# Splitting the keys of four attention blocks per image, in a three-layer attention kernel on one core

## The chip, the core and the metric

The kernel runs on one core of a Trainium2 chip. Five engines work side by side: TensorE (PE, its weight loads PEld), VectorE (DVE), ScalarE (ACT), GpSimd (POOL) and SyncE (SP), which issues most transfers. They meet only at semaphores. The metric is the device time of one execution in microseconds.

## The reference

The input is two images of 32 by 32 tokens with 128 channels. Three layers follow one another, each with a residual:

```
x = LN(x + gate * proj(neighbourhood attention 7x7, 8 heads))   # per image, zero-centred q, k, v
u = LN(x);  h = tanh(q[i] + k[j] + bh), 32 units wide
t = x + softmax_j(h . Wa) @ u                                    # all 1024 keys j of the image
t = t + FFN of one expert in eight, chosen by argmax of LN(t) @ gate_w, capacity 320 tokens
```

The middle layer is the costly one: for each query and each of 1024 keys of its image a tanh over 32 hidden units, 2 x 1024 x 1024 x 32 values. The first layer needs for a block of 128 tokens (4 image rows) the keys of at most 10 rows. The middle layer needs the first layer's result of all the image's tokens as keys, and of one block as queries.

## The kernel before, in words

Tokens are cut in 16 blocks of 128, eight to an image.

**Rounds.** The first layer runs in rounds rho = 0 to 31, two for a block (even and odd heads). A round is: four score products on TensorE (L601), four biased scores with their minimum on VectorE (`bias_score`, L1125), four exponentials on ScalarE (L986), two or three groups of four transposes (L630 or L639), their copies (L993, L1144, L1152), and value products (L648). After a block's second round the heads are normalized, projected and gated. Rounds 0 to 15 (image 0) run by themselves at the start.

**The passage.** Then the layer norms of rows 4 to 7 run on VectorE in one chain (`row_stats`, `scale_start`, `scale_end`, `normal_rows`, `weigh_rows`), tokens are transposed (`turn_tokens`), and the keys k4 and the queries q4 are projected.

**Units.** The middle layer runs in 128 units, eight to a block. A unit is a tile `ring[t % 3]` of 128 x 4096: four tiles of 1024 keys, each with another query column q4[:, m] added. GpSimd adds to keys in SBUF (`key_query_sums`, L507) and VectorE to a copy of the keys in PSUM (L1323): in image 0 GpSimd writes 2 x 1024 + 2 x 512 columns and VectorE 2 x 512; in image 1 GpSimd 2 x 1024 + 512, VectorE 512 + 1024. ScalarE takes one tanh over all 4096 columns (L1049), and TensorE sums over the hidden units (`energies`, L801) into PSUM banks 0 and 1. Sums for unit t are written while step t - 2 runs, and may not overtake `h_used` of unit t - 3.

**The end of a block.** After its eighth unit VectorE takes the minimum over 1024 energies (`least`, L1330; TensorE waits for it before the next block's first energies), ScalarE the exponential (L1053), TensorE transposes and attends (L813, L822), and VectorE normalizes, routes and numbers the tokens (L1349 to L1393) over the next steps. GpSimd scatters the record (L515).

**The order.** Every engine's program is one loop over steps t. Fixed functions of t say what it does: `begin(rho) = 3 * (rho - 17)` starts rounds 16 to 31 every third step, from -3 to 42, and `values_step`, `project_step` and `query_block` follow from it and from the block's end. Image 1's layer norms of rows 12 to 15 lie at steps 49 to 55 or so, and its keys have to be there at unit 64. After unit 127 the expert layer runs.

## Time and profile before

| | us |
|---|---|
| median of 3 runs | 742.11 |
| lowest, highest | 741.74, 746.65 |
| the profiled execution | 744.08 |
| its span | 741.9 |

The span is that of one profiled execution, from its first to its last instruction; 2.2 us of that execution's time lie outside. Busy shares are PE 77%, ACT 78%, DVE 75%, POOL 63%. The execution has four parts: the first image's rounds and the passage up to the first tanh at 109.8 us; units 0 to 63 with the second image's rounds between them, up to 421.8; units 64 to 127, up to 659.9; and the expert layer.

### The profile page before, as it was taken

To read this page: it belongs to the slowest core of one execution; us is meant where nothing else is said; L and a number is where in the kernel's file an instruction comes from. 1 tells how busy PE (TensorE), PEld (TensorE's weight loads), DVE (VectorE), ACT (ScalarE), POOL (GpSimd) and SP (SyncE) were. 2 spreads that over 40 slices of the span, in tenths; PEclk is the share of its full clock that TensorE was granted. 3 is DMA by queue.
4 is the path that set the end of the run, shared out by engine and by line. 5 is a ranking of instruction groups with operands and counts; after the bars stand their busy time and mean duration, and the time that the engine had idled before them with its cause. 6 is when DMAs were issued, how large, how long until landed. Compare 5 with 4: busy or idle time off the path is not lost.

```text
span 741.9 us, 12240 instructions
## 1 busy us (share of the span) xinstructions
PE 570.2 (77%) x4496; PEld 272.5 (37%) x4496; DVE 555.0 (75%) x1444; ACT 577.5 (78%) x368; POOL 470.6 (63%) x539
## 2 busy tenths in 40 slices
PE   6999858798999868899447666766767668768994
PEld 3666423243434323343113131222222212328783
DVE  3768765768897768878987788798798786853356
ACT  3777539998999767899457899999999999960541
POOL 2000228976888668788835788788888886830464
PEclk9999968999999869999858899999999998986998
DMA  8500000000000000007000000000000000001400
GB/s 322 175 1 2 1 0 2 0 2 4 9 4 10 3 9 5 1 12 285 21 4 8 4 11 2 12 9 4 12 10 4 12 8 5 6 7 25 133 22 28
DMA packets 13819, 22.22 MB, mean 30 GB/s; under 512 B 1264, under 2 KB 11026, under 8 KB 12992
## 3 DMA queue, kind: packets, MB, share of 16 engines
q1 hardware_dynamic: 12352, 18.53, 7.3%
q0 software_dynamic: 1408, 2.91, 1.2%
q8 instruction: 36, 0.59, 0.3%
q14 instruction: 23, 0.19, 0.1%
HBM read 14.70 MB, written 7.37 MB: 30 GB/s over the span
## 4 chain that ended last, share of the span: by engine, by line
PE 36%; DVE 27%; issue 18%; ACT 13%; POOL 4%; DMA 0%; DVEq 0%; POOLq 0%; SPq 0%; ACTq 0%
PE ps L801 12%; ACT front L1049 11%; DVE front L1323 7%; POOL front L507 4%; PE ps L601 3%; PE ps L946 3%; PE ps L936 2%; PE ps L648 2%; PE ps L822 2%; DVE back L1125 2%; PE ps L630 2%; PE ps L639 2%; DVE lnw L134 1%; PE ps L813 1%; DVE rec L1362 1%
## 5 line engine op out<-in xcount | busy, mean ns | idle before, releaser
L507 POOL TENSOR_SCALAR front<-k,q 128x1024 f32<-128x1024 f32 (+1 forms) x448 | 410.9, 936 | 129.0 <-PE ps L801 110.7
L1049 ACT ACTIVATE front<-front 128x4096 f32<-128x4096 f32 x128 | 456.2, 3608 | 41.8 <-DVE front L1323 23.6
L801 PE MATMUL ps<-front,cst 128*32 128x512 f32 x2048 | 277.1, 648 | 74.8 <-ACT front L1049 61.1
L1323 DVE TENSOR_SCALAR front<-ps,q 128x512 f32<-128x512 f32 (+1 forms) x256 | 213.5, 877 | 34.6 <-PE ps L801 27.9
L801 PEld LDWEIGHTS ps<-front,cst 128*32 128x32 f32 x2048 | 53.1, 114 | 173.6 <-issue 85.2
L986 ACT ACTIVATE back<-back,mn 128x320 f32<-128x320 f32 (+1 forms) x128 | 62.5, 537 | 20.2 <-DVE mn L1125 20.2
L1125 DVE CUSTOM_DVE_ANT_0 back<-ps,back 128x320 f32<-128x320 f32 (+1 forms) x128 | 54.0, 468 | 12.8 <-PE ps L601 11.8
L464 POOL TENSOR_SCALAR y_all<-y_all,lny,lnc 128x128 f32<-128x128 f32 x8 | 3.5, 444 | 69.0 <-DVEq L1224 69.0
L1338 DVE COPY ptm<-ps 128x512 f32<-128x512 f32 x32 | 22.1, 689 | 30.1 <-PE ps L813 30.1
L1152 DVE COPY back<-ps 128x512 f32<-128x512 f32 x44 | 30.2, 687 | 16.3 <-PE ps L639 13.9
L639 PEld LDWEIGHTS ps<-cst,back 128*128 128x128 f32 x176 | 20.0, 150 | 44.0 <-issue 31.6
L832 PE MATMUL ps<-cst,rec 128*128 128x128 f32 x16 | 5.9, 371 | 38.0 <-DVE rec L1362 38.0
L822 PEld LDWEIGHTS ps<-x_one,ptm 128*128 128x128 f32 x256 | 31.4, 199 | 10.0 <-issue 8.8
L822 PE MATMUL ps<-x_one,ptm 128*128 128x129 f32 x256 | 34.3, 289 | 0.8 <-DVE ptm L1338 0.8
L515 POOL DMA_INDIRECT xbuf<-rec,slots x16 | 16.3, 1019 | 29.2 <-DVEq L119 25.9
L639 PE MATMUL ps<-cst,back 128*128 128x128 f32 x176 | 31.3, 303 | 2.2 <-DVE back L1152 2.0
L543 POOL DMA_INDIRECT out<-back,dest x20 | 19.9, 993 | 17.6 <-DVE back L1529 13.4
L630 PE MATMUL ps<-cst,back 128*128 128x128 f32 x176 | 27.3, 287 | 1.7 <-ACT back L993 1.7
L601 PE MATMUL ps<-late 32*128 32x320 f32 (+1 forms) x128 | 26.7, 494 | 2.5 <-DVE mn L1125 1.7
L813 PEld LDWEIGHTS ps<-cst,pm 128*128 128x128 f32 x128 | 14.7, 151 | 32.8 <-issue 19.2
L813 PE MATMUL ps<-cst,pm 128*128 128x128 f32 x128 | 22.9, 306 | 4.7 <-ACT pm L1053 2.0
L1072 ACT ACTIVATE front<-ps 128x384 f32<-128x384 f32 (+1 forms) x8 | 3.1, 434 | 29.8 <-PE ps L926 29.8
(140 smaller groups left out, 701.4 us busy)
## 6 DMA issues: line engine op xcount, KB each, us to landing
back<-in_w SPq DMA_DIRECT2D x2, 2048.0 KB, 10.3
xbuf<-rec SPq DMA_DIRECT2D x1, 2720.0 KB, 14.4
front<-xbuf SPq DMA_DIRECT2D x2, 720.0 KB, 7.2
back<-in_inner SPq DMA_DIRECT2D x1, 1280.0 KB, 9.8
back<-in_b SPq DMA_DIRECT2D x1, 1280.0 KB, 14.1
xT<-in_xT SPq DMA_DIRECT2D x4, 256.0 KB, 5.4
back<-in_top SPq DMA_DIRECT2D x1, 1024.0 KB, 6.8
back<-in_bottom SPq DMA_DIRECT2D x1, 1024.0 KB, 14.9
```

The costliest lines, as they stand in the source:

```text
L507: last = nc.gpsimd.tensor_scalar(ring[t % 3][:, c, lo:hi], k4[:, img * L + lo:img * L + hi], q4[:, m:m + 1], 1.0, ALU.add, ALU.mult)
L601: return nc.tensor.matmul(bank(to, 0, n), q_par[img][r][rows, at * P:(at + 1) * P], kT[img][rows, k0:k0 + n], start=True, stop=True)
L630: last = nc.tensor.transpose(bank(turn_bank(rho, c), g * P, (g + 1) * P), prob[r][:, g, c * P:(c + 1) * P], c_("ident"))
L639: last = nc.tensor.transpose(bank(4, g * P, (g + 1) * P), prob[rho % 2][:, g, c * P:(c + 1) * P], c_("ident"))
L801: last = nc.tensor.matmul(bank(half)[c * U:(c + 1) * U, :], c_("wa", U - QPG - QPG * s, 2 * U - QPG - QPG * s), ring[t % 3][:, c, half * 5 ...
L813: last = nc.tensor.transpose(bank(4, k * P, (k + 1) * P), pm[:, (4 * half + k) * P:(4 * half + k + 1) * P], c_("ident"))
L822: last = nc.tensor.matmul(bank(6, 2 * P, 2 * P + C + 1), ptm[:, k, :], x_one[:, p // BPI * BPI + k, :], start=(k == 0), stop=(k == BPI - 1))
L986: nc.scalar.activation(prob[r][:, g, 0:n], nlog[r][:, g, 0:n], ACT.Exp, bias=mn[r][:, g:g + 1], scale=-1.0).then_inc(p_ready, 1)
L1049: nc.scalar.activation(ring[t % 3], ring[t % 3], ACT.Tanh).then_inc(h_ready, 1)
L1125: nc.vector.tensor_tensor_reduce(out=nlog[r][:, g, 0:n], in0=bank(frm, 0, n), in1=btab[kind][:, 2 * g + r, :], scale=-1.0, scalar=3e38, op ...
L1152: nc.vector.tensor_copy(pts[rho % 2][:, c, :], bank(4)).then_inc(turn_copied, 1)
L1323: last = nc.vector.tensor_scalar(ring[t % 3][:, c, lo:hi], ps[:, at + lo:at + hi], q4[:, m:m + 1], None, ALU.add)
```

## The change: what it does

- Only rounds 0 to 11 run by themselves. Rounds 12 to 31 lie in the step loop, which begins at step -6, at steps given by a table: -6, -3, 0, 2, then 7 to 35 every fourth, then 38 to 59 every third.
- The units are cut in groups. In each image blocks 0 to 3 first take the 512 keys of the image's first half (four units a block, eight tiles of 512 keys), then, again four units a block, the other 512; blocks 4 to 7 take all keys as before. So units 0 to 15 need only the tokens of blocks 0 to 3; the second half's keys are made at step 14 and used from unit 16. There are 128 units as before. In image 1 the first half's keys are made at step 61 and the second's at about 75.
- Energies of a half group go to one bank, block by block in turn, and TensorE waits for the minimum of the group before the last rather than of the last. The minimum and the shifted energies of the first half are kept in `pmh` and `nmh`; the exponential is in two instructions then.
- In second halves ScalarE makes the eighth tile itself, from the keys with the query as its bias, so a unit has a tanh of 3584 columns and one of 512, and VectorE has one sum less.
- In half units GpSimd writes six tiles of 512 in image 0 and five in image 1; VectorE two and three, less the one of ScalarE in second halves.
- Layer norms of rows 0 to 3 come earlier among the rounds. Those of rows 4 to 6 and of row 7 are separate chains inside steps 7 to 12, on VectorE, with rows 4 to 6 weighed by GpSimd.
- q, k and v of the first layer have one buffer (`conv`) instead of two, overwritten at steps 4 to 9.

```diff
-PACE = 3
+RS = 12
+BS = RS // 2
...
+BEGIN = dict(zip(range(RS, NR), [-6, -3, 0, 2] + [7 + 4 * k for k in range(8)] + [38 + 3 * k for k in range(8)]))
+ROWS_STEPS = (7, 8, 9)
+ENTRY = 4
+KEYS_1, TOKENS_2, KEYS_2 = 14, 58, 61
...
+        self.block, self.half, self.first, self.units = block, half, first, units
+        self.last = first + units - 1
+
+
+GROUPS = []
+for _img in range(B):
+    for _half in range(2):
+        for _k in range(BPH):
+            GROUPS.append(Group(_img * BPI + _k, _half, len(GROUPS) and GROUPS[-1].last + 1, CH // 2))
+    for _k in range(BPH, BPI):
+        GROUPS.append(Group(_img * BPI + _k, None, GROUPS[-1].last + 1, CH))
+GROUP_AT = [n for n, g in enumerate(GROUPS) for _ in range(g.units)]
+FINAL = {g.block: n for n, g in enumerate(GROUPS) if g.half != 0}
+PEND = [GROUPS[FINAL[p]].last for p in range(NB)]
+
+
+def tiles_of_unit(u):
+
+    g = GROUPS[GROUP_AT[u]]
+    k = u - g.first
+    base = g.block * U
+    if g.half is None:
+        return [(c * L, 0, L, base + c * CH + k, k, c) for c in range(QPG)]
+    return [(n * HL, g.half * HL, HL, base + n % QPG * CH + 2 * k + n // QPG, 2 * k + n // QPG, n % QPG)
+            for n in range(2 * QPG)]
...
+def leasts_before(n):
+
+    return n if GROUPS[n].half is None or (n and GROUPS[n - 1].half is None) else n - 1
...
-        late = sb("late", [P, 3 * L + VB * NH * HP])
-        q_par, kT, vals = [], [], []
-        for t in (front, late):
-            q_par.append([t[:, r * L:(r + 1) * L] for r in range(2)])
-            kT.append(t[:, 2 * L:3 * L])
-            vals.append(t[:, 3 * L:3 * L + VB * NH * HP].rearrange("p (n h d) -> p n h d", n=VB, h=NH))
-        ring = [front[:, i * QPG * L:(i + 1) * QPG * L].rearrange("p (c j) -> p c j", c=QPG) for i in range(3)]
+        conv = sb("conv", [P, 3 * L + VB * NH * HP])
+        q_par = [conv[:, r * L:(r + 1) * L] for r in range(2)]
+        kT = conv[:, 2 * L:3 * L]
+        vals = conv[:, 3 * L:3 * L + VB * NH * HP].rearrange("p (n h d) -> p n h d", n=VB, h=NH)
...
+        NEW_KEYS = [0, 4 * BPH, T // 2, T // 2 + 4 * BPH]
+
+        def pool_part(u, n):
+
+            g = GROUPS[GROUP_AT[u]]
+            if g.half is not None:
+                return (0, HL) if n < (6 if g.block < BPI else 5) else (0, 0)
+            if g.block < BPI:
+                return (0, L) if n < 2 else (0, HL)
+            return (0, L) if n < 2 else (0, HL) if n == 2 else (0, 0)
+
+        def biased(u):
+
+            return GROUPS[GROUP_AT[u]].half == 1
...
+                if u in NEW_KEYS:
+                    pool.wait_ge(k4_ready, 1 + NEW_KEYS.index(u))
+                    pool.wait_ge(q4_ready, 1 + NEW_KEYS.index(u))
+                for n, (at, k0, keys, m, _, _) in enumerate(tiles_of_unit(u)):
+                    lo, hi = pool_part(u, n)
+                    if lo < hi:
+                        last = nc.gpsimd.tensor_scalar(ring[u % 3][:, at + lo:at + hi],
+                                                       k4[:, img * L + k0 + lo:img * L + k0 + hi], q4[:, m:m + 1],
+                                                       1.0, ALU.add, ALU.mult)
                 last.then_inc(pool_sums, 1)
...
+                if t == 8:
+                    scale_rows(2, 4, 7)
+                    weigh_rows("lng", ALU.mult, 4, 7)
+                    weigh_rows("lnb", ALU.add, 4, 7, done=True)
+                if t == 11:
+                    normal_rows(2, 4, 7)
...
+                    if t == g.first and leasts_before(n) > 0:
+                        pe.wait_ge(least_ready, leasts_before(n))
+                tiles = tiles_of_unit(t)
+                for at, _, keys, _, row, c in (tiles if keys_whole(t) else tiles[half * QPG:(half + 1) * QPG]):
+                    to, at = (half, at + half * HL) if keys_whole(t) else (g.block % 2, at)
+                    last = nc.tensor.matmul(bank(to)[c * U:(c + 1) * U, :],
...
+                if t == begin(RS) + 1:
+                    spread(BS - 1)
+                    turn_tokens(0, 0)
+                if t == begin(RS) + 2:
+                    project(BS - 1)
+                    key_half(0, 5)
+                    query_columns(0, 1)
...
+                if t == KEYS_1:
+                    pe.wait_ge(n_ready, NG * (RPI + 2))
+                    turn_tokens(1, 2)
+                    query_columns(1, 3)
+                    pe.wait_ge(dve_sums, NEW_KEYS[1])
+                    key_half(1, 5)
...
+                if biased(t):
+                    at, k0, keys, m, _, _ = tiles_of_unit(t)[-1]
+                    k0 += GROUPS[GROUP_AT[t]].block // BPI * L
+                    if t in NEW_KEYS:
+                        act.wait_ge(k4_ready, 1 + NEW_KEYS.index(t))
+                        act.wait_ge(q4_ready, 1 + NEW_KEYS.index(t))
+                    nc.scalar.activation(ring[t % 3][:, 0:at], ring[t % 3][:, 0:at], ACT.Tanh)
+                    nc.scalar.activation(ring[t % 3][:, at:at + keys], k4[:, k0:k0 + keys], ACT.Tanh,
+                                         bias=q4[:, m:m + 1]).then_inc(h_ready, 1)
+                    return
...
+                    nc.scalar.activation(pm[:, 0:HL], pmh[:, p % BPI, :], ACT.Exp, bias=nmin[:, :], scale=-1.0)
+                nc.scalar.activation(pm[:, lo:L], pm[:, lo:L], ACT.Exp, bias=nmin[:, :], scale=-1.0).then_inc(pm_ready, 1)
...
+                if half is None and img == 0:
+                    base -= HL
+                if half == 1 and img == 0:
+                    base -= HL
+                for n, (at, k0, keys, m, _, _) in enumerate(tiles_of_unit(u)):
+                    lo = pool_part(u, n)[1]
+                    if lo < keys and not (biased(u) and n == 2 * QPG - 1):
+                        last = nc.vector.tensor_scalar(ring[u % 3][:, at + lo:at + keys],
+                                                       ps[:, base + k0 + lo:base + k0 + keys], q4[:, m:m + 1], None, ALU.add)
                 last.then_inc(dve_sums, 1)
...
+                if g.half == 0:
+                    k = p % BPI
+                    if p >= BPI:
+                        dve.wait_ge(pm_ready, k + 1)
+                    nc.vector.tensor_tensor_reduce(out=pmh[:, k, :], in0=bank(p % 2), in1=c_("ba").broadcast_to([P, HL]),
+                                                   scale=-1.0, scalar=3e38, op0=ALU.add, op1=ALU.min,
+                                                   accum_out=nmh[:, k:k + 1]).then_inc(least_ready, 1)
...
+                if g.half == 1:
+                    link(nc.vector.tensor_tensor_reduce(out=pm[:, HL:L], in0=bank(p % 2), in1=c_("ba").broadcast_to([P, HL]),
+                                                        scale=-1.0, scalar=3e38, op0=ALU.add, op1=ALU.min,
+                                                        accum_out=nml[:, :]))
+                    nc.vector.tensor_tensor(nmin[:, :], nml[:, :], nmh[:, p % BPI:p % BPI + 1],
+                                            ALU.min).then_inc(least_ready, 1)
+                    link.end()
...
+                if t == KEYS_1:
+                    tokens_out(1, 2)
+                    dve.wait_ge(q4_done, 2)
+                    nc.vector.tensor_scalar(q4[:, P:2 * P], bank(3, 0, P), c_("bh"), None, ALU.add).then_inc(q4_ready, 1)
+                    keys_out(1, 5)
+                if group_end(t) is not None:
+                    least(group_end(t))
                 if 0 <= t + 2 < T:
...
+                if t == project_step(6) + 1:
+                    dve.wait_ge(misc_read, misc_uses(t))
+                    row_stats(4, 7)
+                    scale_start(4, 7)
+                    scale_end(4, 7, ln_scale)
+                if t == project_step(6) + 3:
+                    dve.wait_ge(ln_rows, 2)
+                    row_stats(4, 7)
+                    scale_start(4, 7)
+                    scale_end(4, 7, ln_last)
+                if t == project_step(7) + 1:
+                    dve.wait_ge(misc_read, misc_uses(t))
+                    row_stats(7, 8)
+                    scale_start(7, 8)
+                    scale_end(7, 8)
+                    normal_rows(y_all, 7, 8)
+                if t == project_step(7) + 2:
+                    weigh_rows(7, 8)
+                    row_stats(7, 8)
+                    scale_start(7, 8)
+                    scale_end(7, 8)
+                    normal_rows(x_all, 7, 8)
```

On GpSimd, where the first units' sums begin. `front` is the ring of sums, `k,q` keys and queries. Before:

```order
L481 TENSOR_SCALAR x_one<-y_all,lny,lnc 128x128 x4
L507 TENSOR_SCALAR front<-k,q 128x1024 x2
L507 TENSOR_SCALAR front<-k,q 128x512 x2
L507 TENSOR_SCALAR front<-k,q 128x1024 x2
L507 TENSOR_SCALAR front<-k,q 128x512 x2
```

And now:

```order
L553 TENSOR_SCALAR x_one<-y_all,lny,lnc 128x128 x4
L574 TENSOR_SCALAR front<-k,q 128x512 x66
L536 TENSOR_SCALAR y_all<-y_all,lny,lnc 128x128 x3
L122 ISA
L543 TENSOR_TENSOR y_all<-y_all,cst 128x384
L122 ISA
L543 TENSOR_TENSOR y_all<-y_all,cst 128x384
L574 TENSOR_SCALAR front<-k,q 128x512 x18
L553 TENSOR_SCALAR x_one<-y_all,lny,lnc 128x128 x3
L574 TENSOR_SCALAR front<-k,q 128x512 x108
```

A unit is six instructions of 512 columns where it was four of 1024 and 512, and rows 4 to 6 are scaled and weighed between the sums of units 10 and 11.

On VectorE, at the end of the layer norm of rows 4 to 7 (`lnw`, `lny`, `lnc` are its small tiles, `x_one` its result). Before, ahead of the first sums of all (L1323):

```order
L133 TENSOR_TENSOR lnw<-lny,lnh 128x4
L134 TENSOR_TENSOR lnw<-lnw,lny 128x4
L135 SCALAR_TENSOR_TENSOR lny<-lnw,lny 128x4
L119 ISA
L1229 TENSOR_SCALAR x_one<-y_all,mvs,lny 128x128 x4
L119 ISA
L1125 ISA back,mn<-ps,back 128x256
L1125 ISA mn 128x1
L1125 ISA back,mn<-ps,back 128x256
L1125 ISA mn 128x1
L1323 TENSOR_SCALAR front<-ps,q 128x512 x2
```

And now, at steps 7 and 8, for rows 4 to 6:

```order
L136 TENSOR_TENSOR lnw<-lny,lnh 128x3
L137 TENSOR_TENSOR lnw<-lnw,lny 128x3
L138 SCALAR_TENSOR_TENSOR lny<-lnw,lny 128x3
L1328 SCALAR_TENSOR_TENSOR lnc<-mvs,lny 128x3
L122 ISA
L1420 ISA pmh,nmh<-ps,cst 128x512
L1420 ISA nmh 128x1
L1408 TENSOR_SCALAR front<-ps,q 128x512 x2
```

The chain stands between the sums of two units, and the next unit's sums and a group's minimum are queued behind it.

On ScalarE, at units 16 and 17, the first of a second half (`back` is the first layer's scores), now:

```order
L1132 ACTIVATE front<-front 128x4096 x2
L1128 ACTIVATE front<-front 128x3584
L1129 ACTIVATE front<-k,q 128x512
L1071 ACTIVATE back<-back,mn 128x320 x2
L1128 ACTIVATE front<-front 128x3584
L1129 ACTIVATE front<-k,q 128x512
```

Each such unit has two instructions where it had one.

## Rows read from the trace of the kernel before

**Rows 1.** The page's first part: busy us, share of the span and instructions.

```profile
PE 570.2 (77%) x4496; PEld 272.5 (37%) x4496; DVE 555.0 (75%) x1444; ACT 577.5 (78%) x368; POOL 470.6 (63%) x539
```

**Rows 2.** Windows of every engine: stretch, its length, busy us (instructions), TensorE clock, DMA.

```profile
0.00:109.70 109.70, 88.10 (x833) 55.65 (x834) 71.62 (x291) 60.30 (x122) 13.33 (x29) 0.93 0.25 85
109.70:250.60 140.90, 124.77 (x1051) 53.20 (x1055) 111.74 (x291) 135.38 (x77) 115.71 (x131) 0.95 0.02 5
250.60:421.70 171.10, 125.00 (x932) 49.96 (x928) 139.94 (x353) 127.20 (x55) 122.48 (x141) 0.84 0.10 38
421.70:659.90 238.20, 166.98 (x1286) 59.20 (x1278) 195.23 (x389) 233.69 (x72) 189.16 (x197) 0.96 0.02 8
659.90:741.90 82.00, 65.34 (x403) 54.48 (x403) 36.45 (x125) 20.88 (x43) 29.96 (x42) 0.86 0.17 48
```

**Rows 3.** Windows of line L1049 (tanh) alone: stretch, length, busy us (tanh units), clock.

```profile
109.70:250.60 140.90, 114.98 (x32) 0.95 0.02 5
250.60:306.80 56.20, 32.52 (x9) 0.82 0.02 5
...
358.30:409.80 51.50, 28.80 (x9) 0.73 0.01 4
```

**Rows 4.** ScalarE's timeline around the first tanh: start, us, what, idle before.

```profile
101.72 0.60 ACT L1003 ACTIVATE xT<-ps 128x512 f32<-128x512 f32 x1 [7.92 <-PE ps L757]
...
109.79 7.14 ACT L1049 ACTIVATE front<-front 128x4096 f32<-128x4096 f32 x2 [0.94 <-POOL front L507]
116.84 0.89 ACT L986 ACTIVATE back<-back,mn 128x256 f32<-128x256 f32 x2
```

**Rows 5.** VectorE's timeline: a round's last copy, then one normalization chain, first and last.

```profile
66.27 0.69 DVE L1144 COPY back<-ps 128x512 f32<-128x512 f32 x1 [0.28 <-PE ps L630]
...
96.71 0.17 DVE L1214 TENSOR_SCALAR lnh<-mvs 128x4 f32<-128x4 f32 x1
...
99.00 0.16 DVE L135 SCALAR_TENSOR_TENSOR lny<-lnw,lny 128x4 f32<-128x4 f32 x1
```

**Rows 6.** Groups by form, 109.7 to 659.9 us: count, busy us, mean ns, idle before.

```profile
L507 POOL TENSOR_SCALAR front<-k,q 128x1024 f32<-128x1024 f32 x254 | 281.2, 1119 | 111.7 <-PE ps L801 110.7
L801 PE MATMUL ps<-front,cst 128*32 128x512 f32 x2032 | 275.2, 649 | 73.6 <-ACT front L1049 59.8 <-DVE nmin L1330 13.5
...
L507 POOL TENSOR_SCALAR front<-k,q 128x512 f32<-128x512 f32 x191 | 130.7, 692 | 0.0
...
L986 ACT ACTIVATE back<-back,mn 128x320 f32<-128x320 f32 x48 | 24.1, 549 | 9.3 <-DVE mn L1125 9.3
...
L1053 ACT ACTIVATE pm<-pm,nmin 128x1024 f32<-128x1024 f32 x15 | 17.0, 1135 | 3.6 <-DVE nmin L1330 3.6
```

**Rows 7.** Groups by form on VectorE, 421.7 to 659.9 us (the second image's 64 units).

```profile
L1323 DVE TENSOR_SCALAR front<-ps,q 128x1024 f32<-128x1024 f32 x63 | 80.2, 1274 | 0.0
L1323 DVE TENSOR_SCALAR front<-ps,q 128x512 f32<-128x512 f32 x63 | 47.0, 746 | 14.1 <-PE ps L801 12.7 <-DVE slots L1393 1.3
```

**Rows 8.** Groups by form on VectorE, 109.7 to 250.6 us (the first 32 units).

```profile
L1152 DVE COPY back<-ps 128x512 f32<-128x512 f32 x28 | 19.3, 688 | 10.1 <-PE ps L639 8.9 <-DVE slots L1393 0.5 <-DVE sv L1355 0.2
L1125 DVE CUSTOM_DVE_ANT_0 back<-ps,back 128x320 f32<-128x320 f32 x38 | 16.9, 482 | 0.0
```

**Rows 9.** VectorE's timeline, the normalization of the second image's last rows.

```profile
361.19 7.01 DVE L134 TENSOR_TENSOR lnw<-lnw,lny 128x4 f32<-128x4 f32 x1
```

**Rows 10.** GpSimd's timeline at the same place.

```profile
351.23 17.62 POOL L507 TENSOR_SCALAR front<-k,q 128x1024 f32<-128x1024 f32 x20
382.40 3.55 POOL L507 TENSOR_SCALAR front<-k,q 128x1024 f32<-128x1024 f32 x4 [13.55 <-PE ps L801]
```

**Rows 11.** TensorE's timeline in the slow stretch after unit 32.

```profile
265.24 1.94 PE L801 MATMUL ps<-front,cst 128*32 128x512 f32 x8 [5.72 <-DVE nmin L1330]
```

**Rows 12.** Windows of 5 us around it: columns as in the second group.

```profile
255.00:260.00 5.00, 4.52 (x36) 2.20 (x32) 4.49 (x15) 2.66 (x3) 4.51 (x6) 1.00 0.00 0
...
265.00:270.00 5.00, 4.76 (x20) 1.15 (x20) 3.08 (x12) 4.64 (x2) 0.00 (x0) 0.50 0.00 0
```

403 lines of the change are left out of this document (196 added, 207 removed).

## The prediction

> **What bounds the kernel now.** I read the page's busy shares first: no engine is above 78% [rows 1], so the bound has to be found part by part. The windows give the four parts [rows 2]. Up to the first tanh (109.8 us) ScalarE is busy for 60. In the first 32 units it is busy for 135.4 of 140.9 us: here ScalarE is the bound, at 96%, with TensorE at 125, GpSimd at 116 and VectorE at 112. In units 32 to 63 it has 127 of 171: 44 us of it are idle. In the last 64 it has 234 of 238. The tail of 82 us is the expert layer.
>
> Two units take 7.05 us from start to start [rows 4], so a unit costs ScalarE 3.53. The lost time of units 32 to 63 sits in two stretches [rows 3]: nine tanh in 56.2 us after 250.6, and nine in 51.5 after 358.3, where the first 32 went at 4.4 each. That is some 17 and, with no rounds left there (9 x 3.6), some 19 us. Both hold layer norms on VectorE. The second shows how: a VectorE instruction on four columns, for which a chain's last takes 0.16 us in the open [rows 5], took 7.01 [rows 9], while GpSimd ran 20 sums without a pause for 17.6 us [rows 10]. Afterwards GpSimd itself idled 13.6 us for want of a free ring tile. In the first stretch TensorE waited 5.7 us for a block's minimum, queued behind such a chain [rows 11]; the granted clock fell from 1.00 to 0.50 (from 2.4 to 1.2 GHz), and eight energy records took 1.94 us [rows 12].
>
> **The change part by part.**
>
> *Up to the first tanh: 109.8 to 84 us.* Round 11's last copy is at 66.3 us now [rows 5]. Ahead of it comes the earlier layer norm of rows 0 to 3: a chain is 2.45 us [rows 5], and with the statistics some 3.5 us are added there. The four scores of round 12, which stood ahead of that copy, leave it (1.7). A second chain follows (2.5), then GpSimd's four rows (1.8), transposes and copy: keys' tokens at about 75.5. Now it is 8.1 us from that copy to the first tanh [rows 4], one GpSimd unit of 3.6 among them. With six sums of 0.69 [rows 6] in place of it and some slack I take 8.5: 84. Bounds: 80, where the norm's chains fit into the rounds' waits, and 95. What is dropped is the passage, in which the layer norm of rows 4 to 7 left ScalarE idle for 7.9 us in one piece [rows 4].
>
> *Units 0 to 31: 140.9 to 158.* ScalarE: 32 x 3.53 = 113; eight rounds (14 to 21) of four exponentials at 0.5 [rows 6] = 16, where ten lie now; three query copies 2; the split tanh. Between 1024 columns (1.135) and 4096 (3.6) a column costs 0.8 ns, so an instruction's fixed part is about 0.3, and 16 more cost 5; exponentials of two or three blocks 3.6. Together 139. GpSimd: 32 x 6 x 0.692 = 133 [rows 6], plus two scatters and the moved rows, also 139, where it had 116. VectorE: sums 16 x 1.49 + 16 x 0.745 = 36; a round's copies and biased scores 4.0 [rows 8], so 32; block ends 8.5 each, which is what the last part leaves beside the sums, (195.2 - 80.2 - 47.0) / 8 [rows 2, 7], so 21; four chains 10 and their surroundings 10. That is 109, hardly less than now. At the 96% of now 139 give 145. On top: the new keys at step 14. From unit 13's tanh it takes energies, transposes and the 8.1 us of above, some 12 in all, against two units that ScalarE has ready (7): 5 lost. And the chains at steps 7 to 12: there VectorE has some 30 us of work in 26, and GpSimd hardly pauses. The ends are 0 and the 19 of the second stretch for each of two pairs; no block ends in these steps, so I take 8. Sum 158.
>
> *Units 32 to 63: 171.1 to 151.* Ten rounds now, where five lay. ScalarE 113 + 20 + 5 = 138. VectorE 48 + 40 + 4.5 x 8.5 = 126, and 10 for the norm of rows 8 to 11: 136. At 96% that is 143. The late layer norm has left this part. That of rows 8 to 11 ends one step ahead of a block's minimum again (step 47 and 48, before 31 and 32), so up to 17 come back; half: 8.
>
> *Units 64 to 127: 238.1 to 258.* Image 1's last norm now falls at steps 66 to 72. ScalarE's work in the first 32 is 113 + 5 + 6 = 124, at the 98% of now 126.5. GpSimd has 32 x 5 x 0.692 = 111. VectorE has three sums a unit until step 79: 2.24 us of 3.53, before chain and block end. The stretch cost 19 with two sums, but with the block end and GpSimd running behind; ends 0 and 25, I take 12.5: 139. The last 32 units are as now, 119.
>
> *The tail* is untouched, 82. The weights' load moves from after step 47 to after step 64, still some 60 units ahead of its use; nothing waits for it.
>
> *Edits at nothing:* `conv` in place of two buffers (its copies are counted above; VectorE is busy for 79% there), and TensorE's weaker wait for minima: it waited 13.5 us in all [rows 6], in full blocks too, which keep that wait.
>
> The sum: 84 + 158 + 151 + 139 + 119 + 82 = 733 us of span. With the 2.2 outside it is 735.2, against 744.1 for the profiled execution. The median lies 2.0 below that one, so the prediction is **733**, 1.2% below 742.1. The gain of 26 us at the start is mostly spent: 17 us on dearer half units, and 20 in the second image, against 20 taken from units 32 to 63.
>
> **Rivals.**
>
> *The stalls stay away* (chance 0.24). The half groups let TensorE go on past a minimum, rounds every fourth step leave VectorE room, and chains away from block ends cost only their 2.45. For it: in the first 32 units of now 96% is reached with VectorE at 79%. Then 82 + 146 + 143 + 128 + 119 + 82 = 700, and I give 705 for the keys' switch. Against it: in half units both GpSimd and ScalarE are full.
>
> *GpSimd becomes the bound and VectorE waits behind it* (0.14, slower). The place is units 3 to 15, the price that of the second stretch. GpSimd needs 4.15 us a unit there and ScalarE 3.53 plus half a microsecond, so GpSimd never pauses by itself. In the trace the pause came when its ring was full, after 17.6 us of sums, and VectorE was blocked for 7.01 of them in one instruction [rows 9, 10]. Each of the two norms, of rows 4 to 6 and of row 7, would cost such an episode, 2 x 19 in place of 8: +30, less two units of GpSimd's lead that come back (8). That gives 755. It decides from 17 us over my 8. The Trainium skill (SBUF — State Buffer, "SBUF: two separate sides") has the mechanism: VectorE and GpSimd share one pair of ports, an exclusive lock for a whole instruction, which a VectorE instruction with two SBUF inputs wants and one that reads PSUM does not. By that rule the change is bad for the norm chains, since half units keep GpSimd's stream dense, while the PSUM sums are unharmed; the trace agrees, with 0.745 us for the sums beside 7.01 for the blocked one.
>
> *The norms cost one episode, or the switch of keys halves the clock* (0.17, no change). TensorE stands for some 5 us at step 14, as it did when the clock fell [rows 11, 12]; energies at twice their time for 10 us give +10. So 743.
>
> *Units don't start early* (0.05). Rows 0 to 3 are normed between rounds on VectorE, and if the chain with GpSimd's share and the two rounds in steps -6 to -1 hold it up, the first tanh comes at 95 or later: 733 + 11 = 744.
>
> The forecast itself has 0.40, with 720 to 746 around it; some 60% of that lies below 734.7. A measurement of this kernel tells 1% (7.4 us) from no change. So faster by over 1%: 0.24 + 0.24 = 0.48; slower: the second rival and tails, 0.20; within 1%: 0.32. The range that leaves out a part of the best and of the worst case is 703 to 757.
>
> **What would show it.** The first tanh at 80 to 88 us, with ScalarE idle for less than 25 us in the 30 before it. Unit 32 at about 242 us and unit 64 at 393. GpSimd above 93% in units 0 to 31. In the VectorE timeline at steps 7 to 12, chains below 5 us each; an instruction of over 3 us there speaks for the slower case. Idle of about 5 us ahead of unit 16. I am wrong if the first 32 units take less than 148 or more than 170 us, or if units 64 to 95 stay at 119.

## The result, and the profile after

The changed kernel is slower: 776.4 us (median of 4 runs, 775.5 to 781.6) beside 742.0 for the kernel before on the same chip, a ratio of 1.047 (interval 1.041 to 1.052). The forecast was 733, with 703 to 757 around it. The profiled execution, with a span of 779.7 us, is the slowest of the four, 5 us above their median. Ratios here and below leave out executions more than 1.5% above the fastest of their kernel; medians are of all executions.

The page of the changed kernel, busy time of each engine and share of the span (before: [rows 1]):

```profile
span 779.7 us, 12538 instructions
PE 591.6 (76%) x4512; PEld 281.1 (36%) x4512; DVE 565.3 (73%) x1503; ACT 578.5 (74%) x395; POOL 504.5 (65%) x673
```

The windows of its stages, cut at the starts of tanh 0, 32, 64 and 96, at the end of tanh 127 and at the end. The columns are those of [rows 2]: the stretch, its length, busy time of TensorE, its weight loads, VectorE, ScalarE and GpSimd, then the granted clock.

```profile
85.10:252.60 167.50, 133.31 (x992) 53.59 (x992) 122.39 (x302) 135.72 (x90) 133.19 (x199) 0.88 0.01 3
252.60:424.20 171.60, 144.50 (x1152) 63.66 (x1155) 145.42 (x401) 137.43 (x77) 124.01 (x145) 0.89 0.02 7
424.20:564.80 140.60, 86.76 (x647) 29.44 (x643) 104.51 (x249) 120.76 (x55) 110.61 (x162) 0.89 0.11 44
564.80:696.90 132.10, 92.85 (x673) 35.16 (x665) 104.50 (x225) 118.16 (x38) 94.09 (x98) 0.90 0.03 8
696.90:779.70 82.80, 65.35 (x403) 54.48 (x403) 36.27 (x125) 20.23 (x44) 29.86 (x42) 0.85 0.17 47
```

| part, us | before | forecast | after | after less forecast |
|---|---|---|---|---|
| to the first tanh | 109.8 | 84 | 85.1 | +1.1 |
| units 0 to 31 | 140.9 | 158 | 167.5 | +9.5 |
| units 32 to 63 | 171.1 | 151 | 171.6 | **+20.6** |
| units 64 to 95 | 119.3 | 139 | 140.6 | +1.6 |
| units 96 to 127 | 118.8 | 119 | 132.1 | **+13.1** |
| tail | 82 | 82 | 82.8 | +0.8 |

ScalarE's busy times were forecast well: 135.7 and 137.4 us in the first two groups of 32 units (139 and 138 in the prediction). VectorE's came out higher, 122.4 and 145.4 us for 109 and 136. Not all of that is work: what its instructions took beyond the shortest record of the same line and shape adds up to some 23 us in units 0 to 31 and 21 in units 32 to 63, an estimate from this trace. In the kernel before it is 7 and 28. What failed is how close to its busiest engine a stretch comes. ScalarE was busy for 96% of the first 32 units before; it now has 81% there, 80% in units 32 to 63 and 89% in the last 32. GpSimd, at 80% in units 0 to 31, is far from the 93% that was to show it as a bound. In units 32 to 63 VectorE has the most, 145.4 of 171.6 us, with TensorE at 144.5.

The start came as forecast. The ScalarE timeline around it (start, length, line, operation, idle before) shows that it still waits, but 3.0 us at the longest, and never for the 7.9 us of [rows 4]:

```profile
74.16 1.01 ACT L1071 ACTIVATE back<-back,mn 128x320 f32<-128x320 f32 x2 [1.27 <-DVE mn L1230]
76.24 0.60 ACT L1088 ACTIVATE xT<-ps 128x512 f32<-128x512 f32 x1 [1.07 <-PE ps L832]
79.71 0.60 ACT L1092 ACTIVATE k<-ps 128x512 f32<-128x512 f32 x1 [1.98 <-PE ps L837]
85.25 7.30 ACT L1132 ACTIVATE front<-front 128x4096 f32<-128x4096 f32 x2
```

The same view at the switch of keys in step 14. ScalarE stood for 4.49 us ahead of unit 15, waiting for VectorE's sums, and for 4.55 ahead of unit 16, the first with new keys: 9.0 us, where 5 had been put down. TensorE's granted clock was 0.69 from 170 to 175 us and 0.62 from 175 to 180, after TensorE had stood for 3.5 us, and 1.00 from 180 to 185. The last two rows are the two-part tanh of the second parts, 3.17 + 0.70 us:

```profile
172.06 3.62 ACT L1132 ACTIVATE front<-front 128x4096 f32<-128x4096 f32 x1 [4.49 <-DVE front L1408]
180.23 3.19 ACT L1128 ACTIVATE front<-front 128x3584 f32<-128x3584 f32 x1 [4.55 <-POOL front L574]
184.85 3.17 ACT L1128 ACTIVATE front<-front 128x3584 f32<-128x3584 f32 x1
187.93 0.70 ACT L1129 ACTIVATE front<-k,q 128x512 f32<-128x512 f32 x1
```

VectorE has five instructions of over 3 us between the first tanh and the end of the last, like that of [rows 9]: 6.78 us at 107.2, 5.24 at 187.1, 3.27 at 255.8, 4.20 at 369.4 and 5.00 at 448.5. The first is a copy of eight values to 256 columns under tanh 5, the fourth the first instruction of the middle norm's second chain, in unit 53.

```profile
107.19 6.78 DVE L1260 COPY rzx<-rz 128x256 f32<-128x256 f32 x1
369.35 4.20 DVE L1319 TENSOR_SCALAR lnh<-mvs 128x4 f32<-128x4 f32 x1
373.58 0.63 DVE L128 TENSOR_SCALAR lnw<-lnh 128x4 int32<-128x4 int32 x1
374.25 0.17 DVE L129 TENSOR_SCALAR lny<-lnw 128x4 int32<-128x4 int32 x1
```

The copy takes 0.32 us in the same place of another profile, that of kernel 7 below, whose instructions up to there are the same:

```profile
109.39 0.32 DVE L1260 COPY rzx<-rz 128x256 f32<-128x256 f32 x1
```

GpSimd's own timeline of the changed kernel, over these two, has nothing but sums. The first run of sums ends at 113.82 us and the copy at 113.97; the second run ends at 374.19 and the instruction at 373.55:

```profile
97.79 16.03 POOL L574 TENSOR_SCALAR front<-k,q 128x512 f32<-128x512 f32 x24
363.61 10.58 POOL L574 TENSOR_SCALAR front<-k,q 128x1024 f32<-128x1024 f32 x12
```

And the windows of three groups of eight units that hold chains or a full VectorE: units 8 to 15, 48 to 55, and the 40 us from unit 64:

```profile
128.00:180.10 52.10, 35.84 (x240) 13.91 (x238) 42.48 (x120) 31.97 (x17) 36.37 (x56) 0.80 0.00 1
336.00:386.20 50.20, 38.71 (x308) 16.86 (x301) 43.22 (x123) 35.24 (x21) 34.58 (x42) 0.86 0.02 5
424.20:464.20 40.00, 23.64 (x190) 9.12 (x182) 37.27 (x90) 30.03 (x10) 29.19 (x45) 0.87 0.36 144
```

In the last VectorE is busy for 93%. That is the late norm of image 1 beside three sums a unit; 5.0 of the 37.3 us are the one held instruction at 448.5.

In units 32 to 63, where the forecast missed most, ScalarE was idle for 34 us. What it waited for, and the longest waits of GpSimd and TensorE (waiting line, releaser, us in all, times, longest):

```profile
ACT front L1132 <- POOL front L574: 14.2, 13, 2.4
ACT back L1071 <- DVE mn L1230: 13.7, 10, 3.4
ACT front L1132 <- DVE front L1408: 3.7, 2, 2.7
POOL front L574 <- PE ps L865: 43.4, 13, 7.2
PE ps L723 <- issue: 15.5, 6, 5.8
```

GpSimd's sums came late, but GpSimd had itself stood for 43.4 us until TensorE's energies freed a tile of the ring, and TensorE for 15.5 at a value product whose releaser the profile does not show. The engines wait for one another in a circle, so that these rows alone name no cause.

For units 96 to 103 the waits of ScalarE and of TensorE:

```profile
ACT front L1132 <- DVE front L1408: 9.3, 7, 1.8
PE ps L892 <- DVE rec L1466: 12.0, 2, 6.3
PE ps L902 <- DVEq L1482: 1.0, 2, 0.5
```

Each unit waits a little for VectorE's sums, and TensorE twice stands some 6 us for a normalized block of VectorE, with its energies queued behind. The blocks of second parts end four units apart, so two block ends, of blocks 10 and 11, reach into units 96 to 106, in which VectorE writes whole keys' sums again. It is the same in units 32 to 39 with blocks 2 and 3. The last 32 units of the kernel before have one block end less, 196 VectorE instructions and 95.9 us for 225 and 104.5:

```profile
541.04:659.86 118.82, 83.06 (x638) 29.58 (x638) 95.94 (x196) 116.94 (x37) 93.16 (x97) 0.96 0.02 7
```

The whole difference of 13.3 us lies in units 96 to 107, 58.1 us for 44.8; units 108 to 127 take 74.0 in both.

### The profile page after: what moved, and what is told of

Its sections match the earlier page's. It is cut to its first block, busy times and chain, and to the rows that moved or that the text cites. A ratio compares the mean times of both kernels' runs of the same rounds, so it can differ in the third digit from the quotient of the medians.

```text
span 779.7 us, 12538 instructions
## 1 busy us (share of the span) xinstructions
PE 591.6 (76%) x4512; PEld 281.1 (36%) x4512; DVE 565.3 (73%) x1503; ACT 578.5 (74%) x395; POOL 504.5 (65%) x673
## 4 chain that ended last, share of the span: by engine, by line
PE 36%; DVE 33%; issue 15%; ACT 13%; POOL 2%; DVEq 0%; DMA 0%; POOLq 0%; SPq 0%; ACTq 0%
PE ps L865 13%; DVE front L1408 9%; ACT front L1128 5%; ACT front L1132 4%; PE ps L675 3%; PE ps L723 3%; DVE back L1230 2%; PE ps L1036 2%; PE ps L714 2%; PE ps L1026 2%; PE ps L639 2%; PE ps L876 2%; ACT front L1129 2%; PE ps L885 1%; DVE lnh L1319 1%
## 5 line engine op out<-in xcount | busy, mean ns | idle before, releaser
L574 POOL TENSOR_SCALAR front<-k,q 128x512 f32<-128x512 f32 (+1 forms) x576 | 441.8, 786 | 143.4 <-PE ps L865 127.8
L1132 ACT ACTIVATE front<-front 128x4096 f32<-128x4096 f32 x96 | 344.4, 3611 | 61.8 <-DVE front L1408 36.0
L865 PE MATMUL ps<-front,cst 128*32 128x512 f32 x2048 | 290.0, 672 | 58.8 <-ACT front L1129 27.4
L1408 DVE TENSOR_SCALAR front<-ps,q 128x512 f32<-128x512 f32 (+1 forms) x256 | 196.7, 810 | 32.8 <-PE ps L865 30.3
L1128 ACT ACTIVATE front<-front 128x3584 f32<-128x3584 f32 x32 | 101.6, 3176 | 5.7 <-POOL front L574 5.7
L1230 DVE CUSTOM_DVE_ANT_0 back<-ps,back 128x320 f32<-128x320 f32 (+1 forms) x128 | 54.3, 468 | 13.7 <-PE ps L675 12.5
L723 PE MATMUL ps<-back,conv 128*32 128x128 f32 x704 | 30.6, 312 | 32.4 <-issue 30.6
L1257 DVE COPY back<-ps 128x512 f32<-128x512 f32 x54 | 37.1, 688 | 23.2 <-PE ps L714 20.1
L1442 DVE COPY ptm<-ps 128x512 f32<-128x512 f32 x32 | 22.0, 688 | 36.2 <-PE ps L876 36.1
L675 PE MATMUL ps<-conv 32*128 32x320 f32 (+1 forms) x256 | 41.4, 477 | 1.7 <-DVE mn L1230 1.5
L714 PE MATMUL ps<-cst,back 128*128 128x128 f32 x216 | 39.1, 308 | 3.1 <-DVE back L1257 3.1
L723 PEld LDWEIGHTS ps<-back,conv 128*32 128x32 f32 x704 | 21.0, 123 | 48.6 <-issue 47.1
L892 PE MATMUL ps<-cst,rec 128*128 128x128 f32 x16 | 5.9, 371 | 33.2 <-DVE rec L1466 33.2
## 6 DMA issues: line engine op xcount, KB each, us to landing
xbuf<-rec SPq DMA_DIRECT2D x1, 2720.0 KB, 14.8
back<-in_bottom SPq DMA_DIRECT2D x1, 1024.0 KB, 15.5
```

What stands on the lines that cost most here:

```text
L574: last = nc.gpsimd.tensor_scalar(ring[u % 3][:, at + lo:at + hi], k4[:, img * L + k0 + lo:img * L + k0 + hi], q4[:, m:m + 1], 1.0, ALU.add ...
L675: return nc.tensor.matmul(bank(to, 0, n), q_par[r][rows, at * P:(at + 1) * P], kT[rows, k0:k0 + n], start=True, stop=True)
L714: last = nc.tensor.transpose(bank(4, g * P, (g + 1) * P), prob[rho % 2][:, g, c * P:(c + 1) * P], c_("ident"))
L723: last = nc.tensor.matmul(bank(6, r * P, (r + 1) * P)[g * HP:(g + 1) * HP, :], vals[:, value_block(j, c), 2 * g + r, :], pts[r][:, c, g * ...
L865: last = nc.tensor.matmul(bank(to)[c * U:(c + 1) * U, :], c_("wa", U - QPG - QPG * row, 2 * U - QPG - QPG * row), ring[t % 3][:, at:at + H ...
L1128: nc.scalar.activation(ring[t % 3][:, 0:at], ring[t % 3][:, 0:at], ACT.Tanh)
```

## Experiments

Two theories stood at the start. **Q**: VectorE's and TensorE's queues, worked in order, are too full for the chains and block ends put into them. **L**: GpSimd's dense sums hold small VectorE instructions off. "Units a to b" are read from the starts of the tanh in each profile; "mended" is kernel 13. The kernel before, measured beside each group of runs, took 743.1 to 745.3 us there (742.0 beside the changed kernel), so runs are compared by their ratios; 0.01 is 7.4 us. Units 32 to 63 took 170.0 to 172.7 us in the profiles of the changed kernel and of 2, 3 and 4, whose edits leave these units alone, so that less than 3 us there says nothing.

**1. The inverse straight from PSUM.** With it nothing in the step that was blocked reads SBUF any more.

```
- reciprocal(rz, bank(7, 0, NH)); tensor_copy(rzx, rz broadcast to 256)
+ reciprocal(rzx, bank(7, 0, NH) broadcast to 256)
```

> Every spread of a block's inverse head sums reads PSUM directly (one reciprocal of 256 columns) instead of a copy from one SBUF tile to another. In the changed kernel two of these copies took 6.78 and 5.24 us where they take 0.29. Theory L (GpSimd's dense stream keeps VectorE's SBUF-to-SBUF instructions out, and that is what the change costs): units 0 to 15 fall from 95 us to about 87 and the whole by 8 to 12 us. Theory Q (VectorE's queue is too long at steps 5 to 15 and where two block ends overlap, and each engine waits for the next in order; who is locked out matters little): no more than 3 us, since the wait moves to the next SBUF instruction.

788.7 us, 1.058 (1.053 to 1.063): 8 us slower than the changed kernel, which neither theory had. Units 0 to 15 took 91.9 us for 95.0. The blocked time is gone and the price has come back as work, as the groups by line show, first of this kernel, then of the changed one (busy, mean ns of one; six of the sixteen copies stand ahead of the first tanh in both kernels, and the other ten took 1.64 us on average):

```profile
L1273 DVE RECIPROCAL rzx<-ps 128x256 f32<-128x256 f32 x10 | 17.5, 1749 | 0.1
```

```profile
L1260 DVE COPY rzx<-rz 128x256 f32<-128x256 f32 x16 | 19.1, 1192 | 2.0 <-DVE rz L1273 0.5
```

A reciprocal pays for each of its 256 columns, 1.75 us, where that of eight takes 0.20. Units 32 to 63 took 183.4 us for 171.6, with VectorE busy for 149.9 us for 145.4: 4.5 us more of VectorE cost 11.8 us of the stretch.

**2. Whole tanh in the second parts.** The change's ScalarE half undone.

```
- return GROUPS[GROUP_AT[u]].half == 1
+ return False
```

> The one part 'ScalarE makes one tile of eight in second halves' is undone: one tanh of 4096 columns there, and VectorE makes the eighth tile. If ScalarE is the bound in second halves (3.69 us a unit in the trace, 3.53 for a whole tanh), 32 x 0.16 = 5 us faster. Theory Q: VectorE gets 32 x 0.75 = 24 us more, in the stretches where two block ends overlap, so 5 to 20 us slower. Theory L: about the same, PSUM sums are not kept out.

787.2 us, 1.058 (1.053 to 1.063), so 8 us slower than the changed kernel, as theory Q had it. ScalarE's biased tile is a gain.

**3. Five half tiles for GpSimd in image 0.**

```
- (6 if g.block < BPI else 5)
+ 5
```

> In image 0's half units GpSimd makes five tiles of eight instead of six, VectorE one more. GpSimd falls from 4.15 to 3.46 us a unit and has pauses. Theory L: units 0 to 15 get faster by 5 to 15 us, no VectorE instruction of over 3 us in them. Theory Q: VectorE gets 0.75 us a unit more in units 0 to 31, the whole is 5 to 15 us slower.

779.4 us, 1.045 (1.040 to 1.051): no different from 1.047, where each theory had expected 5 to 15 us, one faster, one slower. GpSimd's busy time in units 0 to 31 fell from 133.2 to 111.1 us, and VectorE's rose from 122.4 to 131.4 by the tile that it took over, so the run is no relief by itself. That GpSimd is not the bound there rests on both: 80% busy with six tiles and 68% with five, at the same time.

**4. Rows 4 to 7 without square roots.** Their statistics and weights stay; the variance stands in for the inverse root.

```
- scale_start(4, 7); scale_end(4, 7, ln_scale)     # and three more pairs
+ scale_none(4, 7, ln_scale)                       # one or two small instructions
```

> The reciprocal square roots of rows 4 to 7 are left out (their rows are scaled by 1, so the output differs): four chains of some 12 small dependent VectorE instructions in steps 7 to 12 become one or two instructions each. Theory Q: units 0 to 15 lose 12 to 18 us of their 95. Theory L: the same, as these instructions took 0.6 instead of 0.16 us there. If the clock or the switch of keys is what costs: under 5 us.

766.3 us, 1.029 (1.022 to 1.035). Units 0 to 15 take 78.4 us where the changed kernel's took 95.0, inside the range of both theories:

```profile
85.60:119.70 34.10, 32.12 (x250) 12.71 (x250) 24.01 (x52) 33.23 (x21) 32.19 (x49) 0.95 0.01 1
119.70:164.00 44.30, 32.51 (x242) 12.70 (x244) 34.83 (x77) 31.81 (x17) 36.14 (x57) 0.85 0.00 1
```

Only half of that is the chains. The profile of kernel 7, whose instructions up to unit 31 are those of the changed kernel, has the same 34.1 us in units 0 to 7 and 51.7 in units 8 to 15:

```profile
87.80:121.90 34.10, 32.15 (x250) 12.71 (x250) 24.00 (x52) 33.25 (x21) 32.17 (x49) 0.95 0.01 1
121.90:173.60 51.70, 34.40 (x242) 13.72 (x244) 42.47 (x121) 31.82 (x17) 36.12 (x57) 0.80 0.00 1
```

So the chains cost 51.7 less 44.3, 7.4 us, where the prediction had 8. With the profiles of the changed kernel, 6 and 12, whose units 8 to 15 have the same instructions and took 52.1 to 54.8 us, it is 8 to 11. The other 8.8 in units 0 to 7 of the changed kernel are the one copy blocked for 6.78 us, which happens in some executions of the same instructions and not in others.

**5. Small operands in PSUM.** The inverse, the logits and the slot sums of a block keep their intermediates in the bank that VectorE reads at that moment.

```
- reciprocal(rz, bank(7, 0, NH)); tensor_copy(rzx, rz broadcast)
+ inv = bank(7, 32, 32 + NH)
+ reciprocal(inv, bank(7, 0, NH)); tensor_copy(rzx, inv broadcast)
...
- lg, oha, over in SBUF
+ plg, poha, pov = bank(7, 40, 40 + NE), bank(7, 48, 48 + NE), bank(7, 56, 56 + NE)
```

> The changed kernel, with the small operands of three chains moved from SBUF to PSUM columns that VectorE owns at that moment, so that these instructions have at most one SBUF input and their SBUF copies none: the spread of the inverse head sums (copies of 6.8, 5.2 and 1.6 us in the trace), the routing and the slot numbers of a block end. Same arithmetic, no instruction more. Theory L (lock-outs are the cost): the waits in these lines go, 15 to 25 us faster. Theory Q (VectorE's queue): units 0 to 7 lose their 8 us, most of it comes back in units 8 to 15, and the whole gains under 8 us. The spread from PSUM alone, by a longer reciprocal (1.75 us each), showed the first half of this: units 0 to 7 35.1 for 42.9, units 8 to 15 56.8 for 52.1.

767.6 us, 1.033 (1.027 to 1.038): 10 us less than the changed kernel for the same arithmetic, between what the two theories had. The ten copies to 256 columns behind the first tanh, 1.64 us on average in the changed kernel, are

```profile
L1275 DVE COPY rzx<-ps 128x256 f32<-128x256 f32 x10 | 4.2, 424 | 0.3
```

The Trainium skill (SBUF — State Buffer, "SBUF: two separate sides") says that VectorE meets GpSimd only on a pair of ports into SBUF that they share, and that the one that starts first keeps the other out for its whole instruction. By that rule an operand in PSUM keeps a small instruction out of the way; the trace agrees, with 0.42 us for each of the ten, where the unblocked copy from SBUF takes 0.29. What still reads SBUF is held as before: in this profile the minimum of two tiles of one column (`nmin`, L1433) took 7.60 us, at 194.6.

**6. A smaller load on VectorE after the block ends.** The tanh of the last half tile takes the query as bias in units 32 to 39 and 96 to 103 too.

```
+ def relieved(u): return g.half is None and g.block % BPI == BPH
+ tanh(ring[:, 0:at]); tanh(ring[:, at:at + HL] <- k4[:, k0:k0 + HL], bias=q4[:, m])
```

> The changed kernel, and ScalarE makes one tile of 512 from the keys also in the eight units after each second half (32 to 39 and 96 to 103), VectorE 512 columns less there. Theory Q says that these units are slow (45.3 and 40.5 us where 34 and 30 would do) because two block ends four steps apart lie on VectorE while its sums are whole again: 8 x 0.65 us less VectorE in each, and the stretches fall by 5 to 9 us each, ScalarE's extra instruction costs 1.3 of it. Theory L, or the half clock as the cause: less than 2 us each, or slower by the 1.3.

773.7 us, 1.038 (1.030 to 1.046). Units 32 to 39 took 40.4 us for 45.3, units 96 to 103 39.0 for 40.5: 4.9 and 1.5 us, where theory Q had 5 to 9 each and L under 2.

**7. Late norms without square roots** (rows 8 to 11, and 12 to 15), as in 4.

> The reciprocal square roots of image 1's rows (8 to 11 at steps 46, 47, 52, 53, and 12 to 15 at steps 68 to 71) are left out, the output differs. Sizes the chains that the kernel before has as well: units 40 to 55 took 88 us and units 64 to 79 77.8. Theory Q: 10 us less in the first, 12 in the second stretch, so 20 us in all. If the stretch 32 to 63 is slow for its ten rounds and not for the chains, the first falls by under 4.

755.8 us, 1.010 (1.004 to 1.016). Units 48 to 55 took 41.4 us for 50.2, units 64 to 79 69.6 for 77.8. But units 40 to 55, the stretch named beforehand, took 82.1 for 88.3, and all of units 32 to 63 165.4 for 171.6: the first norm's chains cost 6 us where 10 were expected, the second's 8 for 12. Of the 22.0 us between the two profiles 10.6 lie in units 0 to 31, whose instructions are the same.

**8. The kernel before with small operands in PSUM**, as in 5.

> The kernel before with the same move of small operands to PSUM. Its lock-outs in these lines are few (the long ones are in the norm chains), so both theories expect under 4 us; more would say that the short waits of 0.5 us count.

740.6 us, 0.996 (0.993 to 0.999). The kernel before gains 3 us by it.

**9. The block end behind the energies.** On TensorE `attend`, `turn_normed`, `logits` and `counts` stand behind the unit's energies.

```
  energies(t, 0); turn_probs_late(...); energies(t, 1)
+ attend, turn_normed, logits, counts        # stood ahead of energies(t, 0)
```

> The changed kernel at 776 us, with one edit on TensorE: in a step, a block's value product of the attention and its three small products for the router stand behind the unit's energies instead of ahead of them. Computes the same. In units 96 to 107 TensorE stood 6.3 and 5.7 us at the product that waits for VectorE's rec (line 1466), with the energies of the unit queued behind it. Theory Q (the block ends four steps apart cost because TensorE's queue holds the energies behind VectorE's chain, which holds back the ring's tiles): units 96 to 111 take 60 to 66 us for 72.2, units 32 to 47 some 5 us less than their 83.4, and the time is 755 to 768. Theory V (VectorE is simply full there, 5 us a unit, whatever TensorE does): units 96 to 111 stay within 3 us of 72 and the time within 5 of 776. Theory C (the half clock of the energies holds the lag): the waits go, but energies still take 3.6 us a unit, and units 96 to 111 gain less than 4.

842.3 us, 1.130 (1.123 to 1.136): theory Q in this form fell badly. Units 96 to 111 took 79.4 us for 72.2, and units 32 to 63, where most of the loss is, 207.8 for 171.6. The waits of ScalarE and VectorE in units 96 to 111, of this kernel:

```profile
ACT front L1132 <- DVE front L1408: 20.0, 9, 5.0
DVE rzm L1453 <- PE ps L885: 10.0, 3, 4.8
```

and of the changed kernel in the same units:

```profile
ACT front L1132 <- DVE front L1408: 11.1, 9, 1.8
```

VectorE is worked in order too. Its part of a block end waits for TensorE's product, which now waits for this unit's tanh, so that VectorE, with the next unit's sums behind it, cannot run ahead of ScalarE. In units 32 to 63 ScalarE waited 36.1 us for VectorE's minima of scores (L1230), for 13.7 in the changed kernel. What looked like TensorE's loss (6 us in front of L892) is the smaller price.

**10. Value products and the rest of the rounds behind the energies as well**, from step 16 on.

```
- values_late, sums_late, spread_late, project_late   # ahead of energies(t, 0)
+ the same, behind energies(t, 1), for t >= 16
```

> As the run before it, and from step 16 on the rounds' value products, sums, spreads and projections stand behind the unit's energies too. Computes the same. The value product (line 723) stood for 3.5 and 5.8 us in units 32 to 63 (9.1 us in units 48 to 55), its energies behind it. Theory Q: units 32 to 63 take 158 to 165 us for 171.6, on top of what the run before it gains; time 742 to 760. Theory V (VectorE is full in units 32 to 63: 145 of 171 us busy): units 32 to 63 within 4 us of 171, time as the run before it.

867.1 us, with a profiled span of 866.4 and a fastest execution of 845.9. No ratio is given, and no more is read from it than that it did not mend the run before: even the fastest is slower than 842.3.

**11. The middle norm one step later.**

```
- middle + 2, + 3, + 8, + 9 (VectorE), + 4, + 5, + 6, + 10 (GpSimd)
+ each one later
```

> The changed kernel, with the two chains of the layer norm of rows 8 to 11, and GpSimd's parts of it, one step later (computes the same), so that the first chain's end stands behind a block's minimum in VectorE's queue and no longer one step ahead of it. Theory Q (the chain keeps the minimum and all behind it waiting): units 48 to 55 take 43 to 47 us for 50.2, time 769 to 774. Leaving the square roots out altogether gave 41.4 there. Theory L (the cost is GpSimd holding VectorE off in the chain's small operations, wherever the chain stands): units 48 to 55 stay at 49 to 52, and the time within 4 of 776.

777.5 us, 1.044 (1.039 to 1.049): unchanged, as theory L had it. Units 48 to 55 took 46.9 us, as Q had it, but units 56 to 63 42.2 for 37.9; together 89.1 for 88.1. Moving the chain behind the minimum moved the loss and did not lessen it.

**12. VectorE relieved in all whole-key units.**

```
- return g.half is None and g.block % BPI == BPH
+ return g.half is None
```

> The changed kernel, and in all 64 units with whole keys (32 to 63, 96 to 127) the tanh of the last half tile takes the query as its bias, so that VectorE writes one sum of 512 columns fewer in each (0.745 us; 24 us over units 32 to 63), for one more ScalarE instruction. Computes the same. VectorE was busy for 145 of 171.6 us in units 32 to 63, TensorE for 144.5, ScalarE for 137. Theory V (VectorE's load is the bound there, and the forecast failed by carrying 96% of ScalarE from a stretch with VectorE at 79% into one with VectorE at 95%): units 32 to 63 take 150 to 160 us. Theory P (TensorE, with its rounds, its half clock and its in-order waits, is): VectorE's busy time falls by 24 us and units 32 to 63 stay above 165. Units 108 to 127, where ScalarE alone is the bound, pay some 0.3 us each for the second instruction, 6 us. Time by V 760 to 770, by P 775 to 785.

768.5 us, 1.035 (1.030 to 1.040). The window of units 32 to 63:

```profile
245.53:410.73 165.20, 139.22 (x1153) 61.40 (x1156) 130.60 (x371) 142.34 (x110) 124.11 (x145) 0.93 0.02 7
```

VectorE has 14.8 us less, not 24, since some of its other instructions take longer, and the stretch is shorter by 6.4. V misses the stretch and P the total: VectorE's load is a part of the loss, at some 0.4 us for each microsecond, and not all of it. The granted clock rose with it, from 0.89 to 0.93, and TensorE's busy time fell by 5.3 us. No run changes the clock alone, so how much of each gain comes by way of the clock is not separated.

**13. Relief in units 32 to 63 and 96 to 107, and small operands in PSUM** (edits of 5 and 12).

> The changed kernel with what helped so far: small operands of spread, route and slot in PSUM, and the tanh with the query as bias in units 32 to 63 and 96 to 107. Computes the same. The first edit alone gave 9 us, the second in 16 of these units 3. Theory V: 747 to 758. Theory P: 761 to 768.

757.5 us, 1.018 (1.015 to 1.022), at the upper end of theory V's range. Units 32 to 63:

```profile
247.83:406.81 158.98, 136.99 (x1159) 61.15 (x1161) 124.40 (x372) 141.37 (x109) 124.02 (x145) 0.95 0.02 8
```

**14. The kernel before with small operands in PSUM and relief in units 32 to 63.** GpSimd takes the lower half of the fourth tile there, ScalarE the upper with the query as bias.

```
+ if 32 <= t < 64:
+     tanh(flat[:, 0:QPG * L - L // 2])
+     tanh(ring[t % 3][:, QPG - 1, L // 2:L] <- k4[:, L // 2:L], bias=q4[:, m:m + 1])
```

> The kernel before, with the same small operands in PSUM (0.9959 of before by itself) and the tanh with the query as bias in its units 32 to 63, where VectorE has 140 of 171 us. Computes the same, with the start and the full keys of before. Theory V: units 32 to 63 lose some 12 to 18 us: 723 to 729, faster than both kernels. Theory P: within 4 us of 740.

**734.3 us, 0.988 (0.984 to 0.991): 1.2% below the kernel before, with an interval that stays under 1.** But it falls between the 723 to 729 of theory V and P's 736 to 744, and the gain is not in its place. Units 32 to 63 of this kernel, and of kernel 8 without the relief:

```profile
249.53:417.26 167.73, 121.69 (x932) 49.98 (x928) 121.74 (x320) 132.49 (x88) 122.44 (x141) 0.87 0.10 39
```

```profile
249.58:418.09 168.51, 118.72 (x932) 48.13 (x928) 139.67 (x352) 126.98 (x56) 122.48 (x141) 0.87 0.10 39
```

18 us of VectorE's time went and 0.8 us of the stretch. The profiled executions of the two kernels are only 2.1 us of span apart, so where the rest of the gain lies these profiles don't tell. In the kernel before these units are held by something else: ScalarE is idle for 35 us there with VectorE at 73%. TensorE's longest waits in them point at it, first of the kernel before, then of this one:

```profile
PE ps L832 <- DVE rec L1362: 20.7, 3, 14.3
PE ps L832 <- DVE rec L1373: 18.7, 3, 12.4
```

The longest wait is for a block's record that stands behind the late norm's chain in VectorE's queue. The chain's instructions were held for 2.81 and 7.01 us in the kernel before and for 3.51, 2.81 and 4.14 here; taking sums away left that as it was. No run took this chain out of the kernel before, so that it is the cause is not shown.

**15. Kernel 13 without the late square roots** (edit of 7).

> The mended kernel (small operands in PSUM, tanh with the query as bias in units 32 to 63 and 96 to 107; 757.5 us) with the square roots of the late layer norms (rows 8 to 11 and 12 to 15) left out: variances stand in for them, statistics, weights and all other work stay. Tells whether the parts of the miss in units 32 to 63 add up. Theory S (they add: VectorE's load and operands 12.6 us, chains 6 to 9, the rest TensorE's and ScalarE's own work): units 32 to 63 take 150 to 154 us for 159.0, units 48 to 55 41 to 43 for 50.0; time 738 to 745. Theory T (with VectorE relieved the chains no longer hold anybody up, or TensorE holds the units by then): units 48 to 55 stay at 46 or more, time 748 to 757.

735.7 us, 0.988 (0.985 to 0.991), for a kernel that leaves the square roots out. Units 32 to 63:

```profile
245.33:394.43 149.10, 135.54 (x1159) 59.96 (x1161) 114.36 (x350) 141.34 (x109) 123.64 (x145) 0.97 0.03 8
```

ScalarE is busy for 95% of it: with VectorE at 77% the stretch is at the rate that the prediction had assumed. Theory T falls; S is nearer, but all three of its ranges were missed on the fast side (149.1 us for 150 to 154, units 48 to 55 39.0 for 41 to 43, the time 735.7 for 738 to 745). The chains cost more here, 9.9 us, than beside a loaded VectorE in 7, where it was 6.2: the parts are not independent.

**16. Kernel 13 with the biased tile in the first parts too.**

```
- return GROUPS[GROUP_AT[u]].half == 1
+ return GROUPS[GROUP_AT[u]].half is not None
```

> The mended kernel again, and in the first parts too (units 0 to 15, 64 to 79) ScalarE takes the last of the eight half tiles from the keys with the query as bias. Computes the same. In units 64 to 71 VectorE was busy for 37.3 of 40 us, in units 0 to 15 for 69 of 87 with GpSimd holding it off. Theory V (VectorE's load): units 64 to 79 take 66 to 71 us for 76.7, units 0 to 15 80 to 85 for 88.9, time 740 to 750. Theory L (what holds units 0 to 15 and 64 to 79 are chains held off by GpSimd's sums, whose number stays): units 64 to 79 stay within 3 us of 76.7, units 0 to 15 within 3 of 88.9, time 754 to 760.

744.8 us, 1.000 (0.998 to 1.003): with the edits of 13 the whole loss of the change made good, and no gain over the kernel before. Units 64 to 71, then 72 to 79:

```profile
402.05:435.36 33.31, 23.52 (x187) 8.86 (x187) 27.13 (x80) 30.81 (x18) 27.74 (x41) 0.92 0.43 173
435.36:472.81 37.45, 20.55 (x152) 6.01 (x148) 24.58 (x64) 29.96 (x17) 30.02 (x44) 0.89 0.01 4
```

Together they take 70.8 us and units 0 to 15 84.4 for 88.9, so that all three of theory V's ranges hold. But the gain is in one place: the first eight took 38.8 us in kernel 13 and gain 5.5, the next eight 0.5. In kernel 13 the norm chain's first instruction was held for 5.0 us in the first eight, and here none is, so that load and hold are not separated.

## Why the prediction was wrong, point by point

*Up to the first tanh* (84; 85.1): right, by the steps given.

*Units 0 to 31* (158; 167.5): the term of the four chains holds, with 7 to 11 us for 8 (experiment 4). ScalarE's term was 3 us too high, 135.7 us for 139, GpSimd's 6, 133.2 for 139, and the switch of keys 4 us too low, 9.0 for 5: that these cancel is luck. VectorE's 109 came out at 122.4. Not foreseen was a single small copy ahead of the chains, blocked in this execution for 6.78 us; where it is not, the same instructions take 156.9, 159.9 and 163.0 us (7, 12 and 6, in the last with another copy blocked for 9.31), beside the 158. The prediction had looked for such an instruction only in the norms. Its sign of over 93% for GpSimd did not fit its own sum, 139 of 158 us or 88%.

*Units 32 to 63* (151; 171.6): **this is the step that failed**, the sentence "At 96% that is 143". The prediction took the 96% from the first 32 units of the kernel before, where VectorE was at 79%, and applied it where its own sum gave VectorE 136 us of those 143, 95%. It measured 145.4, of which some 21 are instructions held longer than their shortest record. With these loads, both feeding a ring of three tiles, ScalarE was busy for 80% and VectorE for 85%. The experiments take the 22.5 us between 171.6 and 149.1 in two steps: 12.6 for VectorE's load and its small operands beside GpSimd's sums (13 against the changed kernel; 6.4 and 4.3 in the profiles with one alone), then 9.9 for the norm of rows 8 to 11 (15 against 13; 6.2 by 7), for which 8 had been put down. With both away the stretch takes 149.1, beside the forecast's 143 without a stall. So the miss of 20.6 us is 12.6 that stood nowhere in the sum, 1.9 on the norm, and 6.1 that remain; of these 3.3 are ScalarE's own work, which is 141.3 us with the relief for the 138 of the forecast. How much of the 12.6 is load, how much being held and how much the clock (0.89, then 0.95) is open.

*Units 64 to 95* (139; 140.6): the place is right, VectorE with three sums, chain and block end, 93% in the first 40 us. The number is partly luck: it was 126.5 without a stall and 12.5 for one. Without the square roots the stretch takes 133.5 (7), so that they cost 7.1, and the biased tile gave back 6 (16 against 13).

*Units 96 to 127* (119; 132.1): "as now" failed. The sums are as now, but the block ends are not: those of blocks 10 and 11 come four units apart and reach into units 96 to 106, one block end more than before in the 32 units, where VectorE again has 2.0 us of sums a unit (0.74 for 512 columns and 1.27 for 1024), for 1.5 in the second parts. The same cost lies in units 32 to 39. It was listed nowhere. Small operands in PSUM take 6 us of it away (125.8 in the profile of 5) and relief in the first eight 3 (129.0 in that of 6); both together leave 126.4, 126.7 and 124.6 (13, 15 and 16), about what the first alone leaves. The other 6 to 8 us stay unexplained: putting the block end behind the energies (9) showed that TensorE's wait for L1466 is not to be had for nothing, and not what the wait costs.

*The tail* (82; 82.8): right.

*The rivals.* The slower one had GpSimd as the bound, with chains blocked behind it in units 3 to 15, for 755. GpSimd was at 80% in units 0 to 31, and a sixth of its work given to VectorE changed nothing (3). Its mechanism, VectorE held off during a dense run of sums, is real: 10 us for the instructions that 5 moved, and five of over 3 us. But in units 3 to 15 it hit a copy of the rounds, and in the norms only single instructions of 0.6 us for 0.16. How it compares with the load itself is not separated, since a held instruction counts as busy. That VectorE's own load could be the bound in whole-key units was in none of the rivals, though its 136 us stood in the sum. The chance of 0.20 for slower was too low for that reason. The third rival's lower clock at the switch came too, for some 10 us. None of the prediction's own signs of being wrong appeared: the first 32 units lay between 148 and 170 us and units 64 to 95 left 119. It had named none for units 32 to 63, except unit 64 at 393 us, which came at 424.

*Where the 25 us of the start went*: 27 into units 0 to 31, 21 into units 64 to 95 and 13 into units 96 to 127 (by the table, after less before), and nothing came back in units 32 to 63, where twice the rounds took the place of the late norm.

Still open: what holds units 32 to 63 of the kernel before, which did not follow VectorE's load (14; the late norm's held chain is the likeliest, untested), and 6 to 8 us of units 96 to 127.

## What to carry to other kernels

Before a rate of the busiest engine is carried from one stretch to another, put every other engine's sum over the time that it gives: ScalarE ran at 95 to 96% beside a VectorE at 77 to 79%, and at 80% beside one at 85%. A step whose sums say "one engine at 96%, another at 95%" has named its own miss. The reverse does not hold: in kernel 14 ScalarE ran at 79% beside a VectorE at 73%, and in units 32 to 63 of kernel 16, where the norm's chains are still there, at 91% beside one at 78%. And a busy share holds the time for which an instruction is held, so compare each small instruction with its shortest record before calling an engine full. When work is moved ahead to fill a start, list what ends later in twos: block ends that came every eight units come every four here, and the units behind them, whose own sums were unchanged, took 13 us more. And in queues that wait for one another, small products ahead of the large one run while it waits; put behind it they made the kernel some 8% slower (1.130 for 1.047).

## What the runs showed of the hardware

A VectorE instruction of 0.29 us took 6.78 us, over ten of GpSimd's sums of 0.67, and one of 0.16 us took 4.20, over nearly five sums of 0.88. So the wait is not over with the GpSimd instruction that is under way. The Trainium skill (SBUF — State Buffer, "SBUF: two separate sides") says that the one that starts first has the pair for its whole instruction; who comes next it does not say, and in these traces it is GpSimd again, up to ten times. In four of the changed kernel's five long ones the wait ends within 0.7 us of the end of a run of sums, after which GpSimd stands 6.5 to 9.3 us for a free tile (runs end at 113.82, 259.73, 374.19 and 453.50 us). Whether such a block comes is a matter of timing: of profiles with the same instructions up to there, some have it under tanh 5 (the changed kernel, 2 and 11, with 42.4 to 42.9 us for units 0 to 7) and some don't (4, 6, 7 and 12, with 34.0 to 34.1). The reciprocal costs 6.8 ns a column, 1.75 us for 256; a copy of as many takes 0.42.
